# State of the decoder's scan turned by VectorE blocks and a DRAM scratch; ln_g and bias passes of GpSimd placed anew

## The reference

```python
x = layernorm(x + attention(x))            # 16 heads of 32, biases, rank-16 updates
x = layernorm(x + q * r)                   # r: per channel r_t = decay * r_(t-1) + ctx_t * ctx_t
x = layernorm(x + ffn(x))
# ffn: quantise rows to 127 levels, ternary w1, silu, gelu, layer_norm * ln_g + ln_b, quantise, ternary w2
```

## Time and profile before

| what | value |
|---|---|
| median of 3 runs | 1043.13 us (1042.7 to 1046.71) |
| the profiled execution | 1045.01 us, span 1043.2 us |
| mean granted clock of TensorE | 0.961 |
| instructions | 23326 |
| busy: PE, DVE, ACT, POOL | 945.8, 909.1, 827.8, 582.7 us |

### The profile page before, as it was taken

The page is one execution under the profiler, slowest core; times in us unless marked ns, Lnnn a source line. Parts: engine busy times, 40 slices in busy tenths (PEclk is TensorE's granted clock), DMA queues, the critical chain, the costliest instruction groups (busy, mean ns, idle before and its releaser), DMA issues.

```text
span 1043.2 us, 23326 instructions
## 1 busy us (share of the span) xinstructions
PE 945.8 (91%) x9260; PEld 647.9 (62%) x9260; DVE 909.1 (87%) x1490; ACT 827.8 (79%) x957; POOL 582.7 (56%) x767
## 2 busy tenths in 40 slices
PE   4898897999999999999999999999999999977415
PEld 3776656676776667676767767676767777654102
DVE  5577878999999999999999999999999999996766
ACT  3556686888889797988989797989889897978684
POOL 3322338374765748484747658484747566572653
PEclk8899998999999999999999999999999999999768
DMA  9423100313122122323132121323131222122214
GB/s 361 156 87 137 43 33 21 74 34 99 25 58 70 49 75 52 84 52 85 21 85 52 55 62 52 84 52 85 52 85 22 71 61 58 42 52 63 53 33 90
DMA packets 106351, 73.67 MB, mean 71 GB/s; under 512 B 91385, under 2 KB 91385, under 8 KB 104450
## 3 DMA queue, kind: packets, MB, share of 16 engines
q1 hardware_dynamic: 105522, 70.34, 24.7%
q10 hardware_dynamic: 720, 1.84, 0.5%
HBM read 41.73 MB, written 8.40 MB: 48 GB/s over the span
## 4 chain that ended last, share of the span: by engine, by line
DVE 32%; PE 29%; ACT 16%; issue 13%; POOL 7%; DMA 3%; SPq 1%; DVEq 0%; ACTq 0%; POOLq 0%
PE bank L1343 9%; PE bank L1482 8%; DVE neg_max L963 6%; POOL h L549 5%; ACT h L725 3%; DVE h L1094 3%; DVE stats L1020 3%; ACT junk L735 2%; ACT h L740 2%; DVE qk_parts L986 2%; DVE fz L1099 2%; PE bank L1483 2%; PE wave L1392 2%; ACT L725 2%; PE wave L1368 2%
## 5 line engine op out<-in xcount | busy, mean ns | idle before, releaser
L963 DVE TENSOR_REDUCE neg_max<-wave 128x8 f32<-128x2048 f32 x64 | 146.1, 2282 | 20.0 <-PE wave L1368 20.0
L549 POOL TENSOR_TENSOR h<-h,g_tile 128x2048 f32<-128x2048 f32 x30 | 139.8, 4660 | 39.1 <-ACT h L740 39.1
L657 ACT ACTIVATE probs<-wave 128x1024 f32<-128x1024 f32 x128 | 124.3, 1024 | 37.8 <-PE wave L1392 37.7
L1482 PE MATMUL bank<-w,xqT 128*128 128x512 fp8e4 x496 | 130.0, 385 | 15.8 <-DMA xqT<-xq 13.0
L439 POOL TENSOR_SCALAR attn_hi<-attn 128x256 fp32r<-128x256 f32 x64 | 28.1, 439 | 176.4 <-DVE attn L1002 161.5
L695 ACT ACTIVATE rows<-rows,rstd 128x512 f32<-128x512 f32 x96 | 74.3, 807 | 41.1 <-POOL rstd L455 23.6
L1094 DVE TENSOR_TENSOR h<-h,b_tile 128x2048 f32<-128x2048 f32 x32 | 84.1, 2630 | 18.6 <-POOL h L549 18.0
L719 ACT ACTIVATE h<-bank,qx 128x512 f32<-128x512 f32 x124 | 82.3, 689 | 19.8 <-PE bank L1483 17.8
L498 POOL TENSOR_TENSOR rows<-rows,bo_tile 128x512 f32<-128x512 f32 x32 | 57.2, 1809 | 71.6 <-DMA rows<-x 71.6
L1489 PE MATMUL bank<-w,hqT 128*128 128x512 fp8e4 x416 | 94.3, 380 | 0.5 <-DMA hqT<-h 0.5
L1482 PEld LDWEIGHTS bank<-w,xqT 128*128 128x128 bf16 x496 | 46.6, 99 | 74.7 <-DMA xqT<-xq 9.9
(11 more groups left out here) (184 smaller groups left out, 2817.9 us busy)
## 6 DMA issues: line engine op xcount, KB each, us to landing
ctx_sb<-ctxT SPq DMA_DIRECT2D x16, 512.0 KB, 3.7
rows<-x SPq DMA_DIRECT2D x16, 512.0 KB, 4.0
out<-rows SPq DMA_DIRECT2D x32, 256.0 KB, 2.5
xT_in<-xT SPq DMA_DIRECT2D x15, 512.0 KB, 4.7
h<-w1T SPq DMA_DIRECT2D x4, 1024.0 KB, 14.3
h<-w2T SPq DMA_DIRECT2D x4, 1024.0 KB, 4.8
h<-Wq SPq DMA_DIRECT2D x1, 1024.0 KB, 6.0
h<-Wk SPq DMA_DIRECT2D x1, 1024.0 KB, 9.7
```

The source lines that it names most:

```text
L549: po.tensor_tensor(h_of(b, q)[:, :], h_of(b, q)[:, :], g_tile[:, :], ALU.mult).then_inc(done, 1)
L657: ac.activation(probs[:, kt, :, :], wave[:, :, kt * T:(kt + 1) * T], ACT.Exp, scale=SM_SCALE).then_inc(S["probs_ready"], 1)
L963: dv.tensor_reduce(neg_max[:, :, :], wave[:, :, :].rearrange("p j (t k) -> p j t k", t=NT), axis=AX_X, op=ALU.max, negate=True).then_inc(S ...
L1482: pe.matmul(p[:, :], xqT[:, q, kc, :], w1[:, kc, n * FW:(n + 1) * FW], start=(kc == 0), stop=False)
```

## The change

- The state is no longer turned by PE. After the clip, DVE transposes it in blocks of 32x32 (two instructions of 128x512) into `x_round`. SP's new `move_state(b)` writes that tile to a DRAM scratch, waits for the write, and reads it back by four transfers, one for each 32 partitions, into `ctx_sb`, where it then lies as rows. `layernorm2_sum` reads it there. The context's channels are laid out in another order in DRAM for this, and the decays with them. `r`, its banks and its signals are gone. `load_ctx` waits for `layernorm2_sum`.
- `half_sum` and `add_halves` are gone; group 0's denominators are made from both halves, as those of the other groups.
- POOL's `g_mul(j-2, 1)` is two halves: one behind `layernorm2_sum(j-1)`, one behind `x_rms(j-1)` and the maxima of group 3; `inverse_std3(j-3, 1)` comes behind the second. `res1(j)` moves to the end of `body(j)`, behind the maxima of batch j+1. `res2(j-2)` waits for the scan's last transpose.
- ACT's `normalise(3, j-3, 1)` moves in front of `probs(j, 3)`.
- SP's order is: `load_xT`, `move_state(j-1)`, `transpose_z(j-3, 1)`, `store_out(j-3, 0)`, `load_ctx(j)`, `store_out(j-3, 1)`, `transpose_x(j-1)`, `load_rows(j)`, `transpose_z(j-2, 0)`.

```diff
+    state_scratch = nc.dram_tensor("state_scratch", (SB, HD, SB, NT * D // SB), F32, kind="Internal").ap()
...
+        state_blocks = flat(x_round[:, :, :])
+        state_rows = flat(ctx_sb[:, :, :])
...
             def load_ctx(b):
-                wait(sp, "rT_ready", b - 1, 2)
+                wait(sp, "ln2", b - 1, 4)
                 if b == 0:
                     sp.wait_ge(u_merge, 5)
                 sp.dma_start(ctx_sb[:, :, :], ctxT[b]).then_inc(S["ctx_loaded"], 16)
+
+            def move_state(b):
+
+                wait(sp, "scan_done", b, 7)
+                wait(sp, "state_moved", b - 1, 16 * SB)
+                sp.dma_start(state_scratch.rearrange("a i s x -> (a i) (s x)"),
+                             state_blocks).then_inc(S["state_out"], 16)
+                wait(sp, "state_out", b, 16)
+                for s in range(SB):
+                    to = state_rows[s * HD:(s + 1) * HD, :].rearrange("p (a x) -> p a x", a=SB)
+                    sp.dma_start(to, state_scratch[:, :, s, :].rearrange("a i x -> i a x")
+                                 ).then_inc(S["state_moved"], 16)
...
+                move_state(j - 1)
                 if alive(j, 3):
                     transpose_z(j - 3, 1)
                     store_out(j - 3, 0)
                 load_ctx(j)
-                transpose_x(j - 1)
                 if alive(j, 3):
                     store_out(j - 3, 1)
+                transpose_x(j - 1)
+                load_rows(j)
                 if alive(j, 2):
                     transpose_z(j - 2, 0)
-                load_rows(j)
...
             def drain():
+                move_state(LAST)
...
+            def g_mul_half(b, i):
+
+                wait(po, "h_normed", b, 2)
+                if b == 0:
+                    po.wait_ge(u_gain, 16 * 2)
+                cols = slice(i * INNER // 2, (i + 1) * INNER // 2)
+                half = h_of(b, 1)[:, cols]
+                po.tensor_tensor(half, half, g_tile[:, cols], ALU.mult).then_inc(S["g_mul"], 1)
...
-                    res1(j - 1)
-                if alive(j, 2):
+                if alive(j, 2):
+                    neg_mean(j - 2, 0)
+                    wait(po, "scan_done", j - 1, 7)
                     res2(j - 2)
-                    neg_mean(j - 2, 0)
                     neg_mean(j - 2, 1)
...
-                    g_mul(j - 2, 1)
+                    wait(po, "ln2", j - 1, 6)
+                    g_mul_half(j - 2, 0)
                 if alive(j, 1):
                     inverse_std2(j - 1)
                     x_rms(j - 1)
+                if alive(j, 2):
+                    wait(po, "shift_split", j, 8)
+                    g_mul_half(j - 2, 1)
                 if alive(j, 3):
                     inverse_std3(j - 3, 1)
                 if alive(j, 2):
...
                     attn_split(j, 3)
                 if alive(j, 2):
                     z_rms(j - 2, 1)
+                if alive(j, -1):
+                    wait(po, "shift_split", j + 1, 2)
+                res1(j)
...
+                    normalise(3, j - 3, 1)
                 if alive(j, 0):
                     probs_of(j, 3)
                 if alive(j, 1):
                     xq_store(j - 1)
                 if alive(j, -1):
                     v_store(j + 1, 1)
-                if alive(j, 3):
-                    normalise(3, j - 3, 1)
...
-            def add_halves(b):
-
-                wait(dv, "probs_ready", b, 2)
-                wait(dv, "xq_stored", b - 2, 1)
-                dv.tensor_tensor(half_sum, probs[:, 0, :, :], probs[:, 1, :, :], ALU.add).then_inc(S["half_added"], 1)
...
+                wait(dv, "scan_done", b, KC + 1)
+                wait(dv, "xq_stored", b - 1, 1)
+                blocks = state_blocks.rearrange("p (s q k c) -> p q k s c", s=SB, q=NT, c=HD)
+                for q in range(NT):
+                    dv.transpose(blocks[:, q, :, :, :],
+                                 ctx_sb[:, :, q * P:(q + 1) * P].rearrange("p k (s c) -> p k s c", c=HD)
+                                 ).then_inc(S["scan_done"], 1)
...
-                wait(dv, "rT_ready", b, q + 1)
+                wait(dv, "state_moved", b, 16 * SB)
                 wait(dv, "norm1", b, q + 1)
-                dv.scalar_tensor_tensor(rows_of(b)[:, q, :], bank_of("r", q, b), SCAN_SCALE, rows_of(b)[:, q, :],
-                                        ALU.add, ALU.mult).then_inc(S["ln2"], 1)
+                state = state_rows.rearrange("p (a q x) -> p q a x", a=SB, q=NT)[:, q, :, :]
+                x_rows = rows_of(b)[:, q, :].rearrange("p (a x) -> p a x", a=SB)
+                dv.scalar_tensor_tensor(x_rows, state, SCAN_SCALE, x_rows, ALU.add, ALU.mult).then_inc(S["ln2"], 1)
...
-                if c == 0:
-                    wait(pe, "half_added", b, 1)
-                    for i in range(GH):
-                        last = pe.matmul(bank[4][i * HD:(i + 1) * HD, T:2 * T], ones[:, :], half_sum[:, i, :],
-                                         start=True, stop=True)
-                for kt in range(NT if c > 0 else 0):
+                for kt in range(NT):
...
-            def r(j, q):
-
-                r_product(take(j, "r", q, "scan_done", j - 1, 5), q)
-
-            def r_product(p, q):
-                for kc in range(KC):
-                    last = pe.transpose(p[:, kc * P:(kc + 1) * P], ctx_sb[:, kc, q * P:(q + 1) * P], ident[:, :])
-                last.then_inc(S["rT_ready"], 1)
...
-                    r(j, 0)
-                    if j == 1:
-                        pe.wait_ge(u_scale, 5)
-                    r(j, 1)
```

More of the change, by code:

```diff
@@ L116, in decoder_kernel @@
         bank += [ctx.enter_context(nc.psum_tensor(f"bank{i}", [P, FW], F32))[:, :] for i in range(GH, 8)]
-        half_sum = x_round[:, :, :].rearrange("p q (i t) -> p (q i) t", t=T)
         sems = {}
@@ L177, in decoder_kernel @@
             (PO, "x_lo", 1), (PO, "attn_split", 8), (PO, "res1", 2), (PO, "res2", 2), (PO, "rstd1", 3),
-            (PO, "rstd2", 4), (PO, "rstd3", 6), (PO, "x_rms", 4), (PO, "h_stat", 8), (PO, "g_mul", 2),
+            (PO, "rstd2", 4), (PO, "rstd3", 6), (PO, "x_rms", 4), (PO, "h_stat", 8), (PO, "g_mul", 3),
             (PO, "z_rms", 4),
@@ L572, in _ @@
             attn_split(0, 3)
+            res1(0)
             def body(j):
[L575 to L576 removed]
                 if alive(j, 2):
+                    neg_mean(j - 2, 0)
+                    wait(po, "scan_done", j - 1, 7)
                     res2(j - 2)
[L579 removed]
                     neg_mean(j - 2, 1)
@@ L609, in body @@
                     z_rms(j - 2, 1)
+                if alive(j, -1):
+                    wait(po, "shift_split", j + 1, 2)
+                res1(j)
             def drain():
-                res1(LAST)
                 neg_mean(PRIOR, 0)
@@ L1057, in quantise_x @@
                 wait(dv, "silu_done", b - 1, 8)
-                if b < NB - 1:
-                    wait(dv, "pv_ready", b + 1, 1)
                 wait(dv, "xqT_loaded", b - 1, 16)
@@ L1086, in z_add @@
                 if b < PRIOR:
-                    wait(dv, "g_mul", b, q + 1)
+                    wait(dv, "g_mul", b, 1 if q == 0 else 3)
                 elif q == 0:
@@ L1521, in drain @@
                 wait(pe, "probs_ready", LAST, 8)
-                wait(pe, "scan_done", LAST, 5)
-                for q in range(NT):
-                    r_product(bank_of("r", q, LAST), q)
                 drain_y(THIRD, 0)
@@ L1700 @@
     put("xT", channels_first(a["x"]))
-    put("ctxT", channels_first(a["ctx_2048"]))
+    put("ctxT", a["ctx_2048"].reshape(NB, T, GH, KC, HD).transpose(0, 2, 4, 3, 1).reshape(NB, P, KC, T))
     for n in "qkvo":
```

31 lines of the change are left out of this document (15 added, 16 removed).

## The result

The changed kernel takes 1095.08 us (median of 4 runs, 1093.41 to 1096.56) against 1043.11 for the kernel before: ratio 1.049, interval 1.0475 to 1.0505. It is slower, as forecast, but by 52 us instead of 28. The profiled execution has a span of 1091.6 us, 48.4 more than before.

What follows compares the result with a forecast made beforehand. It took PE (57.17 of 57.53 us busy) and an equally long ring through ACT's shift_rows as bounds. 12 x 2.3 = 27.6, plus 1.5 for iteration 15, minus 1.7 at the ends: +27.4, giving 1071 us, range 1058 to 1081.

Steps and rivals of the forecast that it cites:

- The step that decides: ACT's normalise before probs(j, 3) waits for POOL's inverse_std3, holding scores(j+1, 0): 59.85 against 57.53, +2.3 us a period.
- The late exponentials: probs(j, 3) on ACT, held by inverse_std3, free PE's banks at 537.45 instead of about 535.2; chance 0.78.
- PE from scores(j+1, 0) to the last f: 15.15: Last term of the period's sum: PE's stretch read from the trace before, 15.05 plus 0.1 us.
- my sum: One period from last f to last f: 27.1 + 4.9 + 9.9 + 2.8 + 15.15 = 59.85 us.
- POOL's small instructions are blocked: Rival: inverse_std3's three instructions wait for DVE's x_round pair, ring 0.3 to 0.9 us longer, 1075 to 1082; chance 0.05.
- PE's wait for `shift_rows`: Sign of being right: at shifted(j, 2) PE also waits for ACT's shift_rows, by a few tenths of a us.
- Iteration 15: Only weighted and xq_store stand behind the late exponentials there: cost between 0 and 3.3 us, taken as 1.5.
- The gain of 1.7 at the ends: State transposes gone from PE: 0.9 us gained in the drain, 0.8 in the first iterations.
- DVE's transposes: Two 128x512 block transposes added on DVE: 0.9 us each if linear in size, 1.8 together.
- PE's sum counts: Rival: PE's load is the bound, late exponentials do not bite; period 56.5, time 1029; chance 0.07.
- ACT's ring holds, no new wait: Rival: POOL reaches inverse_std3 by 531.7 as now; period 57.3 to 57.5, 1038 to 1042; chance 0.08.
- The state comes late: Rival: the DRAM round trip needs over 20 us; at 25 us the sums start 3.2 late, 1109; chance 0.02.

Runs made afterwards that it cites:

- experiment 1: Kernel after with ScalarE's normalise(3, j-3, 1) put back behind v_store(j+1, 1): 1056.32 us, ratio 1.0116 to the kernel before.
- experiment 2: Kernel before with only normalise(3, j-3, 1) moved in front of the last exponentials: 1044.05 us, ratio 1.0004.
- experiment 11: Kernel after with inverse_std3(j-3, 1) before half 0's wait: 1057.01 us; also h_norm behind shiftT(j, 2): 1055.67; also inverse_std2 before half 0: 1054.18.
- Experiment 3: Kernel after with 20 unused 128x256 products on PE in the wait before scores(j+1, 0): 1073.28 us, ratio 1.028 to the kernel before.
- Experiment 6: Kernel before with only POOL's second ln_g pass halved and placed as in the kernel after: 1053.37 us, ratio 1.0097.
- experiment 7: Kernel after with POOL's g_mul(j-2, 1) whole, in its old place, without the wait for the sums: 1110.04 us, ratio 1.0636 to the kernel before.
- the control in 8: Kernel before with only ACT's h_norm(j-2, 1) moved behind shiftT(j, 2): 1043.76 us, ratio 1.0.
- experiment 12: z_max of row tile 0 over half its columns (part of the maximum left out): in the kernel before 1041.14 us, in experiment 11's third kernel 1052.28.
- experiment 9: Kernel after, normalise(3, j-3, 1) in its old place, half 0 without its wait: 1072.21 us; also h_norm(j-2, 1) behind shiftT(j, 2): 1071.68.
- experiment 5: Kernel after with inverse_std3(j-3, 1) in front of the ln_g pass's second half: 1072.74 us, ratio 1.0273 to the kernel before.

## Why the prediction was right in its direction and wrong in its size

**The step that decides: right.** The late exponentials were most of the cost. Position by position behind the last `f`, which ended at 511.13: `y(j, 1)` ends at 537.92, 26.8 (forecast 27.1); the second-norm sums take 4.9 more, as forecast; POOL from there to `inverse_std3` 10.4 (forecast 9.9); ACT 2.8, as forecast. `scores(j+1, 0)` starts at 44.97, forecast 44.8. Experiments 1, 2 and 11 show the mechanism from three sides: undo the move, do it without the late POOL, do it with POOL early.

**The step that failed: "PE from scores(j+1, 0) to the last f: 15.15".** It was read from a trace in which PE had not been idle, and measured 572.49 - 556.10 = 16.39, 1.24 more. Behind its own 2.3 us wait PE ran at the lower of its two levels, granted clock 0.50 and 0.54 (1.2 instead of 2.4 GHz), for two groups of products: (1.93 + 1.84) - (1.07 + 1.05) = 1.65 us by their durations. The clock fell 0.7 to 1.1 us after PE had started again, in each of the twelve periods. Experiment 3 shows it: fill the idle time, and the period is 59.90 with a clock of 1.00, and 21.8 us go, 1.8 a period. With the clock kept, my sum was right to 0.1 us, in part by luck: `scores` started at 45.05 there (547.99 - 502.94; the four terms in front of it add up to 44.7), and the last step took 14.85 instead of 15.15. I could have seen it: the kernel before shows the same once, in its start, behind a wait of 3.49 us for the same exponentials:

```profile
90.91 0.98 PE L1368 MATMUL wave<-qk_parts 32*128 32x256 f32 x24 [3.49 <-ACT probs L657]
91.82 1.75 PE L1406 MATMUL bank<-probs,v_sb 128*32 128x256 f32 x16
```

1.75 us for the group that takes 1.07 elsewhere; from 91.8 to 93.5 the granted clock was 0.58. I forecast an idle PE and priced what came behind it at full clock.

**The small terms.** `inverse_std3` took 1.6 instead of 1.2: two of its steps last 0.81 and 0.40 beside DVE's rounding, the rival "POOL's small instructions are blocked", which I gave 0.05, at its lower half; it made 0.4 of the 3.79. PE's wait for `shift_rows`, forecast at a few tenths, was 0.8. Iteration 15 cost 3.2 instead of 1.5. The gain of 1.7 at the ends was 0.2. DVE's transposes took 1.30 instead of 1.8, the state's two transfers 2.6 and 2.8 from issue to landing: covered, as forecast. Twelve periods at 3.79 instead of 2.3 are 18 of the 24 to 25 us missed, the ends and iteration 15 another 3. The rest, 3.6, is that the median of before lies 1.9 below its profiled execution and that of after 1.7 above.

**The rivals.** *PE's sum counts* is refuted: no kernel that keeps the state off PE has a mean period under 58.35 us. *ACT's ring holds, no new wait* has the right condition and the wrong time: without the wait for a late `inverse_std3` (experiments 1 and 11) the kernel takes 1054 to 1057, not 1038 to 1042. What I missed there is that half 1 of the ln_g pass, and what follows it on POOL, falls beside DVE's quantisation. Experiment 6 prices the halves in their new places at 10 us without any other part of the change. In it and in experiment 1 two of DVE's quantising products are longer than before in nearly every period. In experiment 1:

```profile
597.63 0.49 DVE L1096 TENSOR_TENSOR qx<-qx 128x2 f32<-128x2 f32 x1
603.36 0.70 DVE L1149 TENSOR_TENSOR fz<-fz 128x1 f32<-128x1 f32 x1
```

Before, the second takes 0.15 us and the first 0.16 in the period of the earlier trace rows. The 0.33 and 0.55 us are nearly all by which the way through DVE has grown, from 24.2 to 25.1. The second ends with POOL's attention split. In experiment 11 it is down to 0.15 again, but another instruction of `quantise_x` (L1105) takes 0.70 instead of 0.25, and the period is the same. So the halves cost by such collisions, and moving POOL's queue only moved them; that they are the whole of the 10 us is not shown, since no run is without them.

And the transposes of the state don't come for nothing: reading it from SBUF instead of a bank makes the second sum exclude POOL's pass (experiment 7), which is why the pass has to wait or the sum does. *The state comes late* is refuted.

**The port.** The traces agree on this: DVE's sum takes 0.68 us on a bank beside POOL's pass, 4.17 and 4.62 with both inputs in SBUF, 1.99 beside the rest of a half. The Trainium skill, page "SBUF — State Buffer", section "SBUF: two separate sides" with its part "Who interferes with whom", says that the loser of the shared pair blocks until the instruction of the other is over, and that a DVE instruction with at most one SBUF input, outside the 2-port modes, does not contend with GpSimd. The traces agree with both: the sum with two SBUF inputs ends 0.55 us behind the pass in experiment 7, and the one on a bank is not lengthened at all. Sentences on that rule stood in the prediction as a reason for the wait in front of half 0; its price for the whole pass, some 3.5 us by experiment 7 (4.17 - 0.68), was not asked for.

## What to carry to other kernels

Where a forecast says that TensorE will wait for some two us, as here, price what runs behind the wait at its lower clock too, and look in the trace of before for a place where it has waited. One period is not the kernel: read the waits over all of them, since a single one here showed a wait for `xqT` where nine of twelve showed one for the silu. Before an operand moves from a bank to SBUF, look which GpSimd pass runs beside its reader: beside one of 4.6 us a sum of 0.68 took 4.17. A kernel with several rings of nearly the same length, 57.2 to 57.6 us here, gains little from any one of them (the control in 8, and 12), and loses by each that grows: 38 of the 52 us hung on where three small GpSimd instructions stand in their queue.

## What the runs showed of the hardware that was not expected

- After 2.29 us without work and another 0.7 to 1.1 us with work TensorE's granted clock fell to 0.50 and 0.54 for 3.5 us, in each of the twelve periods; behind the waits of 0.9 and 1.0 us of experiment 1 it was 1.00. Adding 2.5 us of useless products a period made the kernel after 2% faster.
- A DVE product of 128x2 elements took 1.80 us (some 0.17 otherwise) and one of 128x8 1.06 us, each ending with the POOL pass beside it: the wait depends on the other instruction's rest, not on the size of the own one.
- A half of the pass, 2.40 us, costs by where it falls: with a few GpSimd instructions more or fewer in front of it, it hit the second sum (1.3 and 1.7 us, experiment 9), the maxima's split (0.9, experiment 12) or the quantisation of x (1.6, experiment 5).
